# A two-layer mixture-of-experts kernel: three input and two output buffers for the layer 0 expert tiles, stores counted one by one, and other times in the table that sets the order

## What is computed

```python
xn = layernorm(x)
x = x + attention0(xn)        # 16 heads of 8, causal softmax over 256
      + ffn0(xn)              # shared silu expert + 2 of 16 experts, F = 64, weights by softmax
xn = layernorm(x)
x = x + attention1(xn)        # delta rule: state = state*(1 - b*k*k) + b*v*k, a scan over 256 tokens,
                              # then layer norm, gate by silu(x @ Wg), out projection
      + ffn1(xn)              # 2 of 4 experts, H = 704, silu(x@w1) * (x@w3) @ w2
```

## Time and profile before

| | |
|---|---|
| median of 3 runs | 2001.16 us (1997.99 to 2007.99) |
| the profiled execution | 2013.11 us |
| its span | 2011.4 us |
| busy: TensorE, VectorE, ScalarE, GpSimd | 78%, 69%, 49%, 45% |
| weight loads of TensorE | 48% |
| granted TensorE clock, mean | 0.865 |

### The profile page before, as it was taken

How to read it: one execution, slowest core, us unless ns; L and a number is a source line. 1 busy time by engine, 2 the same in 40 slices (tenths; PEclk the granted TensorE clock), 3 DMA queues, 4 the chain that set the end, 5 groups by cost and what they waited for, 6 DMA issues and landing times.

```text
span 2011.4 us, 29786 instructions
## 1 busy us (share of the span) xinstructions
PE 1567.2 (78%) x9764; PEld 967.2 (48%) x9766; DVE 1395.0 (69%) x2664; ACT 978.3 (49%) x1600; POOL 905.1 (45%) x973
## 2 busy tenths in 40 slices
PE   2953977898777998888654887999999988698950
PEld 2840444454444554444332554656666655465530
DVE  5775655676555776776677855788888878787822
ACT  2721545565444665445444544556665644455410
POOL 4247437725543224658786265111111257621126
PEclk9875979998776999778776888999999989999985
DMA  6954678888655765656445374565665657665423
GB/s 207 291 150 140 197 196 232 246 224 225 193 163 169 207 176 139 160 151 191 114 130 183 111 214 151 162 187 172 172 185 170 185 181 230 200 179 167 131 80 90
DMA packets 277946, 354.44 MB, mean 176 GB/s; under 512 B 32272, under 2 KB 204304, under 8 KB 272416
## 3 DMA queue, kind: packets, MB, share of 16 engines
q1 hardware_dynamic: 237600, 287.92, 50.4%
q0 software_dynamic: 17056, 33.66, 5.8%
q10 hardware_dynamic: 23136, 30.94, 4.5%
HBM read 197.48 MB, written 122.68 MB: 159 GB/s over the span
## 4 chain that ended last, share of the span: by engine, by line
PE 43%; DVE 15%; issue 14%; ACT 8%; POOL 6%; DMA 5%; SPq 4%; another core or an unknown queue 4%; ACTq 0%; DVEq 0%; POOLq 0%
PE Y L1062 7%; PE R L819 5%; PE R L821 5%; PE R L820 5%; PE R L835 3%; POOL xs_dram L1368 3%; DVE state L2024 3%; PE Y L957 3%; PE R L922 2%; ACT probs L1535 2%; PE R L895 2%; DVE row_max L1923 2%; DVE acc_in L1749 2%; DVE dw L2018 2%
## 5 line engine op out<-in xcount | busy, mean ns | idle before, releaser
L1923 DVE TENSOR_REDUCE row_max<-R 128x6 f32<-128x768 f32 x256 | 241.3, 953 | 133.3 <-PE R L922 65.8
L1388 POOL TENSOR_TENSOR o_acc<-o_acc,read 128x512 f32<-128x512 f32 x112 | 143.9, 1284 | 408.4 <-DVE read L2034 407.5
L1368 POOL DMA_INDIRECT xs_dram<-sc_in,pos x256 | 269.4, 1052 | 109.5 <-issue 63.6
L1347 POOL DMA_INDIRECT gat<-ys_dram,pos x256 | 253.8, 992 | 133.2 <-issue 68.0
L1379 POOL TENSOR_SCALAR_AFFINE_SELECT probs<-probs 128x512 f32<-128x512 f32 x256 | 167.7, 655 | 316.6 <-ACT probs L1535 312.6
L1062 PE MATMUL Y<-hid,fd 128*128 128x512 f32 x456 | 250.0, 630 | 35.2 <-DVE hid L2072 26.5
L1535 ACT ACTIVATE probs<-R 128x768 f32<-128x768 f32 x256 | 205.0, 808 | 137.6 <-PE R L945 91.9
L819 PE MATMUL R<-fhl,fw 128*128 128x512 f32 x418 | 231.8, 555 | 19.2 <-issue 5.1
L2072 DVE TENSOR_TENSOR hid<-R,sil 128x512 f32<-128x512 f32 x228 | 155.7, 686 | 60.1 <-ACT sil L1654 24.4
L2024 DVE TENSOR_TENSOR_SCAN state<-dw 128x512 f32<-128x512 f32 x128 | 172.3, 1346 | 16.2 <-issue 7.9
L1654 ACT ACTIVATE sil<-R 128x512 f32<-128x512 f32 x190 | 112.9, 595 | 140.1 <-PE R L821 103.0
(11 more groups left out here) (270 smaller groups left out, 3479.7 us busy)
## 6 DMA issues: line engine op xcount, KB each, us to landing
fw<-wf SPq DMA_DIRECT2D x38, 1408.0 KB
q_rows<-kq SPq DMA_DIRECT2D x128, 256.0 KB
fx<-xs_dram SPq DMA_DIRECT2D x86, 256.0 KB
xs_dram<-gat SPq DMA_DIRECT2D x24, 512.0 KB, 4.6
qk_dram<-qk_parts SPq DMA_DIRECT2D x32, 384.0 KB
Q<-qk_dram SPq DMA_DIRECT2D x64, 192.0 KB
K<-qk_dram SPq DMA_DIRECT2D x64, 192.0 KB
fw<-wf SPq DMA_DIRECT2D x96, 128.0 KB
```

Of the source, the lines that this page charges most:

```text
L1347: pool.indirect_dma_start(gat[:, i % 2, 2 * t + a, :], None, ys_dram[l][g], bass.IndirectOffsetOnAxis(ap=pos[l][g][a][:, col:col + 1], axi ...
L1368: pool.indirect_dma_start(xs_dram[g], bass.IndirectOffsetOnAxis(ap=pos[l][g][a][:, col:col + 1], axis=0), sc_in[:, n % 2, t * P:(t + 1) * ...
L1923: dve.tensor_reduce(row_max[:, b, h2, :, :], pair[:, :].rearrange("p (g c t) -> p g c t", g=2, t=P)[:, :, 0:3, :], AX.X, ALU.max).then_inc ...
```

## The change

Four things:

- fx0 and fw0 have three buffers (F0_BUFS) and fy0 two. LF0 of tile n waits for FD0 of tile n - 3; ScalarE's evacuation of tile n waits for the store of tile n - 2.
- c_saved becomes x1_saved, x1n_saved and xT1_saved, one count for a chunk each. C1 waits for x1_saved of the chunk before, C1b for x1n_saved, C2 for xT1_saved; LS of layer 1 waits for x1n_saved alone, LD for xT1_saved alone, and LDx now waits for x1_saved.
- In the table `soon` is 4.4 (from 2.8), the load of a layer 0 tile takes 2.7 on the sync queue, lands in 8.0 (from `soon` + 1) and is due 12 (from 7) ahead of the tile; a scatter or gather takes 1.28 on GpSimd (from 1.03).
- The waits declared in the table follow the code.

```diff
-    soon, later = 2.8, 6.0
+    soon, later = 4.4, 6.0
...
-                stage(t + every * i + every * k / 8, "SC", m, k, after=after, POOL=1.03)
+                stage(t + every * i + every * k / 8, "SC", m, k, after=after, POOL=1.28)
...
-            after = since(f, 2, ("FD0", 0, "PE"))
+            after = since(f, F0_BUFS, ("FD0", 0, "PE"))
...
-            stage(t - 7, "LF0", f, after=after + [("RC4", 0, g, "DVE")], SP=2.0)
-            stage(t, "FT0", f, after=[(("LF0", f, 0, "SP"), soon + 1)], PE=0.55,
+            stage(t - 12, "LF0", f, after=after + [("RC4", 0, g, "DVE")], SP=2.7)
+            stage(t, "FT0", f, after=[(("LF0", f, 0, "SP"), 8.0)], PE=0.55,
...
-        fx0 = sb("fx0", [P, 2, TILES, P])
+        fx0 = sb("fx0", [P, F0_BUFS, TILES, P])
...
-        fy0 = sb("fy0", [P, C])
-        fw0 = sb("fw0", [P, 2, 2, W0E])
+        fy0 = sb("fy0", [P, 2, C])
+        fw0 = sb("fw0", [P, F0_BUFS, 2, W0E])
...
-                    if n >= 2:
-                        sp.wait_ge(*bank_of["fy0", n - 2].filled())
-                    sp.dma_start(fx0[:, par, :, :].rearrange("p (s t) d -> p s (t d)", s=2),
+                    if n >= F0_BUFS:
+                        sp.wait_ge(*bank_of["fy0", n - F0_BUFS].filled())
+                    sp.dma_start(fx0[:, n % F0_BUFS, :, :].rearrange("p (s t) d -> p s (t d)", s=2),
...
-                    if n >= 1:
-                        act.wait_ge(*f0_saved(n - 1))
+                    if n >= 2:
+                        act.wait_ge(*f0_saved(n - 2))
...
                 if kind == "LD":
-                    sp.wait_ge(*c_saved(n))
+                    sp.wait_ge(*xT1_saved(n))
...
                 if kind == "LDx":
+                    sp.wait_ge(*x1_saved(n))
...
                 if kind == "C1":
                     dve.wait_ge(*acc_loaded(n))
                     if n >= 1:
-                        dve.wait_ge(*c_saved(n - 1))
+                        dve.wait_ge(*x1_saved(n - 1))
```

More of the change, by code:

```diff
@@ L271, in scatter @@
             m = l * NCH + n
-            saved = [(("SAx", n, 0, "SP"), soon)] if l == 0 else [(("C1b", n, 0, "ACT"), soon), (("SC1", n, 0, "SP"), soon)]
+            saved = [(("SAx", n, 0, "SP"), soon)] if l == 0 else [(("C1b", n, 0, "ACT"), soon)]
             stage(t + every * i - 4, "LS", l, n, after=saved + since(m, 2, ("SC", 2 * TILES - 1, "POOL"), lag=soon),
@@ L302, in experts0 @@
             stage(t + 2, "FD0", f, after=[("FU0", f, 0, "DVE")], PE=0.6,
-                  ACT=(1.05, since(f, 1, ("FD0", 0, "ACT"), lag=soon)))
+                  ACT=(1.05, since(f, 2, ("FD0", 0, "ACT"), lag=soon)))
             banks("FD0", f, 0, ("FD0", f, 0, "ACT"), 2)
@@ L381, in sums0 @@
                 after = [(("FD0", sum(NT[0][:g + 1]) - last, 0, "ACT"), soon) for last in (1, 2)] if k == 0 else []
-                stage(t + 1.2 * k, "CG", n, k, after=after + (free if k == 0 else [("CG", n, k - 1, "POOL")]), POOL=1.03)
+                stage(t + 1.2 * k, "CG", n, k, after=after + (free if k == 0 else [("CG", n, k - 1, "POOL")]), POOL=1.28)
             stage(t + 12, "C1", n, after=[(("CL", n, 0, "SP"), soon), (("CG", n, 2 * TILES - 1, "POOL"), soon)]
-                  + since(n, 1, ("C1b", 0, "ACT"), ("SC1", 0, "SP"), lag=soon), DVE=4.1, POOL=pow4)
+                  + since(n, 1, ("C1b", 0, "ACT"), lag=soon), DVE=4.1, POOL=pow4)
             stage(t + 16, "C1b", n, after=[("C1", n, 0, "POOL")], DVE=0.1, ACT=2.1)
-            stage(t + 18, "C2", n, after=[("C1b", n, 0, "ACT")], PE=0.55, ACT=(whole, since(n, 1, ("C3", 0, "PE"))), DVE=odd)
+            stage(t + 18, "C2", n, after=[("C1b", n, 0, "ACT")], PE=0.55,
+                  ACT=(whole, since(n, 1, ("C3", 0, "PE")) + since(n, 1, ("SC1", 0, "SP"), lag=later)), DVE=odd)
             banks("C2", n, 0, ("C2", n, 0, "DVE"))
@@ L438, in delta @@
         for n, t in enumerate(d):
-            after = [(("SC1", n, 0, "SP"), soon), (("C1b", n, 0, "ACT"), soon)] + since(n, 1, ("D0", 0, "PE"), ("D0b", 0, "PE"), ("D1g", 0, "PE"))
+            after = [(("SC1", n, 0, "SP"), later)] + since(n, 1, ("D0", 0, "PE"), ("D0b", 0, "PE"), ("D1g", 0, "PE"))
             if n == 0:
@@ L472, in delta @@
             banks("D1g", n, 0, ("D1g", n, 0, "DVE"))
-            stage(t + 35, "LDx", n, after=[("LD", n, 0, "SP")] + since(n, 1, ("SD", 0, "SP"), lag=soon), SP=issue)
+            stage(t + 35, "LDx", n, after=[(("C1b", n, 0, "ACT"), soon), ("LD", n, 0, "SP")] + since(n, 1, ("SD", 0, "SP"), lag=soon), SP=issue)
             stage(t + 40, "D3a", n, after=[("DS", n, HD - 1, "POOL")], PE=0.4, ACT=(whole, since(n, 1, ("D3d", 0, "DVE"))),
@@ L495, in sums1 @@
                 after = [(("FZ1", sum(NT[1][:g + 1]) - last, 0, "ACT"), soon) for last in (1, 2)] if k == 0 else []
-                stage(t + 1.1 * k, "EG", n, k, after=after + (free if k == 0 else [("EG", n, k - 1, "POOL")]), POOL=1.03)
+                stage(t + 1.1 * k, "EG", n, k, after=after + (free if k == 0 else [("EG", n, k - 1, "POOL")]), POOL=1.28)
             stage(t + 10, "E1", n, after=[(("EL", n, 0, "SP"), soon), (("EG", n, 2 * TILES - 1, "POOL"), soon)], DVE=2.4)
@@ L894, in _ @@
                         to = slice(s * S, (s + 1) * S)
-                        ins = pe.matmul(bank[:, to], fw0[:, par, s, 0:2 * F0], fT0[:, par, to], start=True, stop=True)
+                        ins = pe.matmul(bank[:, to], fw0[:, n % F0_BUFS, s, 0:2 * F0], fT0[:, par, to], start=True, stop=True)
                     ins.then_inc(bank.full, 1)
@@ L902, in _ @@
                         to = bank[:, (t // 2) * C + (t % 2) * P:(t // 2) * C + (t % 2 + 1) * P]
-                        ins = pe.matmul(to, hid0[rows, par, t * P:(t + 1) * P], fw0[rows, par, t // 2, 2 * F0:W0E],
+                        ins = pe.matmul(to, hid0[rows, par, t * P:(t + 1) * P], fw0[rows, n % F0_BUFS, t // 2, 2 * F0:W0E],
                                         start=True, stop=True)
@@ L1570, in _ @@
                         act.wait_ge(*bank_of["r1", n - 1].filled())
-                        act.wait_ge(*c_saved(n - 1))
+                        act.wait_ge(*xT1_saved(n - 1))
                     act.activation(xhl1[:, 0, :], bank[:, :], ACT.Copy).then_inc(x_hi[1].sem, 1)
```

24 lines of the change are left out of this document (13 added, 11 removed).

## The result

| | before | after |
|---|---|---|
| median, us (4 runs each) | 2003.39 (1997.99 to 2007.99) | 1901.38 (1900.32 to 1906.27) |
| ratio | | 0.9497, 95% interval 0.9466 to 0.9527 |
| span of the profiled execution, us | 2011.4 | 1899.5 |
| granted TensorE clock, mean | 0.865 | 0.880 |

102 us were won. The forecast was 49 against the profiled execution and 51 against the median, and its range ended at 1917: the sign was right, the size was half of what came.

What follows compares the result with a forecast made beforehand. TensorE was taken to bound only part of the time (1567 of 2011 us). Terms -9 - 13 - 17 - 8 - 2 = -49 gave 1964 against 2013.1, less 12 for the median: 1952 us; 8-in-10 range 1917 to 1994.

Steps and rivals of the forecast that it cites:

- Start, -9: Kernel start: VectorE's constants moved earlier, so TensorE's first router matmul comes at about 28.4 us; -9 us.
- Start of the attention, -13: 100 to 205 us: first masking behind fewer scatters, row maxima transferred sooner, less a new wait of some 6; -13 us.
- 205 to 980, -17: 205 to 980 us: third input buffer, longer load leads and separate stores remove TensorE's waits; -17 us.
- The queue's wait at the tile load: Sign for 205 to 980 us: the sync queue's wait at layer 0 tile loads, 77.7 us, falls under 40.
- TensorE's share of the window: Sign for 205 us on: TensorE's busy share rises over 86%.
- 980 to 1110, -8: 980 to 1110 us: kl goes ahead of layer 0's last sum on VectorE, shortening TensorE's 25.2 us wait; -8 us.
- Layer 1, -2: 1610 us to the end: layer 1's sums stand one or two places later on VectorE beside the tiles; -2 us.
- (a): Rival, 980 to 1110 us: GpSimd's full queue gives back half of the earlier gains; 1972, up to 1985; 18%.
- (b): Rival: only named waits go, longer leads bring nothing of their own; 1984, or 1975 with the start; 8%.
- (c): Rival: group 0's scatters give way to maskings, layer 0 tiles start over some 15 us later; +15, 2016; 8%.
- (d): Rival: due order holds the load back, third buffer never used; some 8 us lost, 1960, within the forecast; no separate chance.
- (e): Rival: the idle time moves, 205 to 980 us gets worse places for what the start wins; 1995 to 2005; 8%.

Runs made afterwards that it cites:

- e8: Before with three moves in its start order (VectorE's constants, ScalarE's first two xhl earlier), no other change; 1987.39 us, ratio 0.9923.
- e1: Before with only the planner's lead of a transfer, soon, at 4.4 instead of 2.8; 1995.73 us, ratio 0.9979.
- e2: Before with only the charge of a scatter or gather on GpSimd at 1.28 instead of 1.03; 1966.26 us, ratio 0.9825.
- e10: All instruction orders of before with the buffers and separate store counts of after; 1921.83 us, ratio 0.9888 (before 1940.04 on that chip).
- e6: After with the charge of a scatter or gather back at 1.03 from 1.28; 1973.04 us, ratio 0.9847 to before.
- f1_after: After itself, unchanged, run again on another chip where before takes 2009.67; 1918.57 us, ratio 0.9535.
- f4: After with only layer 1's scatters and gathers charged 1.03 again; 1950.23 us, ratio 0.968 to before.
- g1: Before with only layer 1's scatters and gathers charged 1.28; 1918.89 us, ratio 0.9894 (before 1940.34 on that chip).
- The singles: Four kernels, each before with one part alone: leads 1995.73, GpSimd charge 1966.26, layer 0 tile buffers and times 1984.85, separate store counts 1984.80 us.

## Why the prediction was right in sign and half in size

Steps as the prediction put them; gains from the table of steps above.

1. *Start, -9.* The mechanism was right: the first router matmul at 28.80, forecast 28.4. The end of the routing came 16 us sooner: 8 by these moves alone (e8), 13 in e1, where the lead makes them together with other moves of the start. So 9 was right for what I had costed, and the other moves were missing. In total e8 gains 16, with an interval of 8 to 23.
2. *Start of the attention, -13.* From routing to tile 23 the gain grew by 33 - 16 = 17. First masking at 144, TensorE busy 73.1 us in 100 to 205: as said. But I had told this part by the planner's 1.03 for a scatter, and e2 with the right charge doesn't move the first masking, while e1 with the lead alone does. The new wait for the third load was 13.5, not 6, and it fell on GpSimd: TensorE lost 2.8 us there.
3. *205 to 980, -17.* From tile 23 to the last masking the gain grew by 65 - 33 = 32. The wait for fw is under 3.0 us, the store wait went, and the row maxima's unnamed wait fell from 19.6 us in this window to 1.4: I had counted a tenth of it. That it was late loads is borne out by e10, where the third buffer frees the sync queue and the unnamed wait is gone with no instruction moved; the leads don't clear it (26.5 us in e1, 40.4 in e6), the charge does most of it (8.2 in e2). Two signs that I named were wrong. The queue's wait at the tile load was 62 us, not under 40: with the loads due 12 us ahead the queue stands again, 4.2 us in the order of before (e10) and 62 in that of after, but TensorE no longer waits for it. And TensorE's share of the window was 646.15 of 775, 83%, not over 86%: the window now held other work, so it was a bad sign.
4. *980 to 1110, -8.* No wait for kl over 15 us: right. The first layer 1 tile gained 71 - 65 = 6 us more than the last masking, near the forecast.
5. *Layer 1, -2.* This is the step that failed: 112 - 71 = 41 us in these two executions, 35 with f1_after in place of after. I had read the charge of 1.28 against one place only, the scatters at 120 us, and had not carried it to the 128 scatters and 128 gathers of layer 1, where delta rule, scatters and tiles share GpSimd. f4 and g1 show that the charge there is the cause of 29 of them; the 6 to 12 left are open, and it stays open by which waits the 29 come about. And I had treated TensorE's 1567 us of busy time as fixed ("the work itself is not changed"). The same matmuls took 1537 us, at a mean granted clock of 0.880 and not 0.865: of the 112 us of span, 30 are shorter busy time, 13 ahead of the first layer 1 tile and 17 behind it.

Together the steps gained 16 + 17 + 32 + 6 + 41 = 112 us where I had 9 + 13 + 17 + 8 + 2 = 49: 39 of the 63 missing are step 5, 15 step 3.

*The rivals.* (a), GpSimd uses it up: in the 128 us ahead of the first layer 1 tile it is as full as before, busy 105 us (909 to 1037) against 98 (980 to 1108), but nothing was given back there. The 71.2 of 130 us in after's window of 980 to 1110 are of other work. (b), only the named waits go and the leads bring nothing: e1 alone seemed to say so, but in after 2.8 costs 38 us and 5.6 is no worse than 4.4. The Trainium skill (DMA: Bandwidth & Descriptors, section Anatomy of one DMA) gives its fit for transfers that GpSimd issues; by it 256 KB would take an estimated 2.6 us. The transfers here go through the sync queue, and 256 KB of xn took a median of 5.0 and 5.4 us in the two profiles of the last section, so the fit doesn't serve as the planner's lead here. (c), slower by late tiles: the first tile is indeed evacuated 11 us later (248 against 238), but tile 23 came 33 us sooner. (d), the third buffer is never used: the sync queue's wait of 4.2 us in e10 says that it is. (e), new waits for the old ones: not in sum.

The singles' gains add to 76 us at the first layer 1 tile (15 + 2 + 28 + 31) where after has 71. That doesn't show that the parts simply add up to there: each is measured from the same execution of before, 10 us above its median, which the sum counts four times. What I had no measure for was the tiles and the stores: by the medians 19 each, where I had 17 for both and for the queue. Some half of that is order, since e10_waits, with the waits of both and no moved instruction, gains 18.

## What to carry to other kernels

In a kernel whose order is fixed by a table of durations, compare every number of the table with the trace at all places where it is used, and fix those that are furthest off together: two such numbers gave 56 us here, against 8 and 37 alone on another chip (between 56 and 45 the runs don't decide, but beside the other edits each is worth clearly more than alone), and the relieved waits 18. Cost a wait on the engine that bounds twice, once as idle time and once as the lower clock behind it; in this case shorter busy time came to about a third of the idle time won (30 beside 82 us). And measure stretches between two steps of the work, since a fixed window of time hides a gain once the work has moved.
